# Two heads in one product: the low-order terms of a linear attention on stacked rows

## The reference

```
qn = _normalize(q) * (scale * temperature)
kn = _normalize(k) * scale
v1 = concat([ones, v]); vN = v1 / N
kv_mod = einsum('bhni,bhnj,bhne->bhije', kn, kn, vN)
kv     = einsum('bhnd,bhne->bhde', kn, vN)
vsum   = sum(vN, axis=-2)
y = A * einsum('bhni,bhnj,bhije->bhne', qn, qn, kv_mod) \
  + scale**2 * Bc * einsum('bhnd,bhde->bhne', qn, kv) + scale**4 * Cc * vsum
y = y[..., 1:] / y[..., :1]
```

## Time and profile before

| | |
|---|---|
| median of 3 runs | 958.41 us (952.2, 959.37, 958.41) |
| the profiled execution | 953.75 us, of which 951.9 us span |
| PE busy | 862.8 us (91%) |
| DVE busy | 645.4 us (68%) |
| ACT busy | 422.1 us (44%) |
| POOL busy | 711.0 us (75%) |
| mean granted TensorE clock | 0.94 |

### The profile page before, as it was taken

One profiled execution on the slowest core, in us unless ns is written; L12 is line 12 of the kernel. 1 busy time (PEld: TensorE's weight loads), 2 busy tenths in 40 slices (PEclk: granted clock), 3 DMA queues, 4 the chain that ended last, 5 costly groups with the idle time before them and its releaser, 6 DMA issues.

```text
span 951.9 us, 20339 instructions
## 1 busy us (share of the span) xinstructions
PE 862.8 (91%) x6492; PEld 533.1 (56%) x6492; DVE 645.4 (68%) x2267; ACT 422.1 (44%) x1156; POOL 711.0 (75%) x498
## 2 busy tenths in 40 slices
PE   3889997897999999999999999999969997599994
PEld 1434443344654554554554555556548986498993
DVE  3699998899487556556456566465886888655552
ACT  3545645333265333333433434344324555266763
POOL 4778878888888888888888888878633156677875
PEclk8699999898899899999999999999979998699997
DMA  9867586436565455445554565563566454578884
GB/s 300 187 134 143 77 166 108 65 42 108 70 123 99 52 85 86 65 42 86 97 86 51 95 102 93 91 124 29 104 199 218 134 193 151 175 125 138 136 134 56
DMA packets 148755, 108.72 MB, mean 114 GB/s; under 512 B 105223, under 2 KB 137162, under 8 KB 148524
## 3 DMA queue, kind: packets, MB, share of 16 engines
q0 software_dynamic: 61344, 26.21, 30.1%
q1 hardware_dynamic: 80800, 70.49, 26.3%
q10 hardware_dynamic: 6508, 10.73, 3.4%
HBM read 65.07 MB, written 42.45 MB: 113 GB/s over the span
## 4 chain that ended last, share of the span: by engine, by line
PE 76%; DVE 16%; issue 3%; DMA 2%; ACT 1%; SPq 0%; DVEq 0%; POOLq 0%; POOL 0%; ACTq 0%
PE ps L1416 15%; PE ps L1205 8%; DVE r2t L1744 6%; PE ps L1629 5%; PE ps L1352 5%; PE ps L1366 5%; PE ps L1640 5%; PE ps L1557 3%; PE ps L1243 3%; PE ps L1252 3%; PE ps L1403 3%; PE ps L1273 2%; PE ps L1392 2%; PE ps L1301 2%; DVE same L1684 2%
## 5 line engine op out<-in xcount | busy, mean ns | idle before, releaser
L748 POOL DMA_INDIRECT edge_sums<-sums,addr x352 | 553.2, 1572 | 126.1 <-issue 100.5
L1781 DVE TENSOR_SCALAR oh<-node,dsrc 128x500 bf16<-128x500 int16 (+1 forms) x448 | 134.5, 363 | 72.5 <-PE ps L1416 71.9
L1416 PE MATMUL ps<-oh,r2t 128*64 128x500 bf16 (+1 forms) x1344 | 146.6, 362 | 1.4 <-DVE oh L1781 1.4
L1003 ACT ACTIVATE r<-ps 128x500 f32<-128x500 f32 (+1 forms) x224 | 103.5, 550 | 80.1 <-PE ps L1352 79.9
L1416 PEld LDWEIGHTS ps<-oh,r2t 128*64 128x64 bf16 x1344 | 70.4, 111 | 72.9 <-issue 33.6
L1744 DVE TENSOR_TENSOR r2t<-ps,r 125x4096 f32<-125x4096 f32 x25 | 110.3, 4412 | 0.0
L1205 PEld LDWEIGHTS ps<-edges,same 128*128 128x128 f32 x704 | 89.3, 199 | 33.3 <-issue 30.1
L1205 PE MATMUL ps<-edges,same 128*128 128x65 f32 x704 | 98.4, 285 | 10.3 <-ACT sums L822 4.7
L793 POOL DMA_INDIRECT out_x<-r x56 | 87.8, 1568 | 26.6 <-DVE r L2179 9.5
L1684 DVE SCALAR_TENSOR_TENSOR same<-srow,src_f,below 128x128 f32<-128x128 int32 x352 | 101.0, 343 | 5.0 <-DMA srow<-in_src_row 5.0
L822 ACT ACTIVATE sums<-ps 128x260 f32<-128x260 f32 x88 | 35.1, 399 | 138.0 <-PE ps L1205 133.3
(11 more groups left out here) (300 smaller groups left out, 1382.4 us busy)
## 6 DMA issues: line engine op xcount, KB each, us to landing
srow<-in_src_row SPq DMA_DIRECT2D x44, 512.0 KB, 5.7
edges<-in_edge_attr SPq DMA_DIRECT2D x22, 512.0 KB
r<-routed_rows SPq DMA_DIRECT2D x56, 129.0 KB
r<-hpre_rows SPq DMA_DIRECT2D x12, 500.0 KB, 4.3
edge_sums<-sums,addr POOLq DMA_INDIRECT x352
r2t<-in_ew SPq DMA_DIRECT2D x4, 1024.0 KB, 10.9
hpre_rows<-r ACTq DMA_DIRECT2D x16, 250.0 KB, 2.6
edge_sums<-r SPq DMA_DIRECT2D x4, 884.0 KB, 13.3
```

What stands on the lines that cost most here:

```text
L748: pool.indirect_dma_start(out=tables[k], out_offset=bass.IndirectOffsetOnAxis(ap=addr[:, j:j + 1], axis=0), in_=sums[:, j % OR, :], in_off ...
L1003: act.activation(phT[:, R % 2, h, 0:n], bank(BP[h], 128, 0, n), ACT.Square).then_inc(pair_squares, 1)
L1416: m = mm(ps[EA * a:EA * (a + 1), BD * BANK:BD * BANK + n], lhsT=parts3[:, (DCH - 1 - 2 * w // DW) * DW + (2 * w + a) % DW, s, :], rhs=oh[: ...
L1781: v.tensor_scalar(oh[:, (2 * i + a) % OHS, 0:nt * P].rearrange("p (t n) -> p t n", t=nt), node16[:, 0:nt, :], dsrc[:, 2 * w + a:2 * w + a ...
```

## The change

The low-order terms of two heads are made by one product of 64 columns over 128 stacked rows: the two heads' queries on rows 0 to 63, their squares on rows 64 to 127. ScalarE builds these rows for both halves of a group, a copy and a square each, four instructions of 64 rows in place of one of 128. TensorE issues two such products, which write different halves of the PSUM rows. VectorE masks the weights in eight pieces of 64x64, which moves them to their rows, in place of two of 128x256.

```diff
-        wlow = sb("wlow", [128, HG, 2, 128])
+        wlow = sb("wlow", [128, HG, 2, 64])
-        R1 = 15800
+        R1 = 16300
-        qsq = carve([128, BW])
+        q_low = carve([128, 2, BW])
@@ q_squares
-                act.activation(qsq[:, 0:n], qnT[:, b % 2, g, 0:n], ACT.Square).then_inc(q2_ready, 1)
+                for a in range(2):
+                    here = qnT[64 * a:64 * a + 64, b % 2, g, 0:n]
+                    act.activation(q_low[0:64, a, 0:n], here, ACT.Copy)
+                    z = act.activation(q_low[64:128, a, 0:n], here, ACT.Square)
+                z.then_inc(q2_ready, 1)
@@ outputs
-                    wait(pe, low_ready, HG)
+                    wait(pe, low_ready, 4 * HG)
                     wait(pe, y_ready, HG * b + g)
                     wait(pe, q2_ready, HG * b + g + 1)
-                    mm(bank(BY, 128, 0, n), lhsT=wlow[:, g, 1, :], rhs=qnT[:, b % 2, g, 0:n], start=True, stop=False, skip_group_check=True)
-                    mm(bank(BY, 128, 0, n), lhsT=wlow[:, g, 0, :], rhs=qsq[:, 0:n], start=False, stop=False, skip_group_check=True)
+                    for a in range(2):
+                        mm(ps[64 * a:64 * a + 64, BY * BANK:BY * BANK + n], lhsT=wlow[:, g, a, :], rhs=q_low[:, a, 0:n], start=True, stop=False,
+                           skip_group_check=True)
@@ before the first gram product
-            pe.wait_ge(low_ready, HG)
+            pe.wait_ge(low_ready, 4 * HG)
@@ VectorE, once
-                v.tensor_tensor(wlow[:, g, :, :], bank(B1, 128, 2 * g * 128, (2 * g + 2) * 128).rearrange("p (a n) -> p a n", a=2),
-                                block[:, :, :].rearrange("p h d -> p (h d)").unsqueeze(1).to_broadcast([128, 2, 128]), ALU.mult).then_inc(low_ready, 1)
+                for a in range(2):
+                    rows = slice(64 * a, 64 * a + 64)
+                    mask = block[rows, 2 * a:2 * a + 2, :].rearrange("p h d -> p (h d)")
+                    for k in range(2):
+                        c0 = (2 * g + 1 - k) * 128 + 64 * a
+                        v.tensor_tensor(wlow[64 * k:64 * k + 64, g, a, :], ps[rows, B1 * BANK + c0:B1 * BANK + c0 + 64], mask,
+                                        ALU.mult).then_inc(low_ready, 1)
```

## The result

The changed kernel takes 964.76 us (median of 16 runs, 960.87 to 969.3), the kernel before 954.89 beside it (16 runs, 949.8 to 960.15): a ratio of 1.010, interval 1.0081 to 1.0118. The forecast was 960.4 with 954.5 to 967: the time lies in the range, but the kernel got slower by 9.9 us where the sum said 2.0. The profiled execution took 968.64 us, with 966.9 of span.

What follows compares the result with a forecast made beforehand. TensorE was taken to bound the attention stage. Its gain of 11.3 us less 5.0, 3.6, 1.8 and 0.7 of waits left about 0.2; with 2.2 for the clock, 958.41 became 960.4 us, range 954.5 to 967.

Steps and rivals of the forecast that it cites:

- round 0: sweep and sums copies: Blocks 1 to 6: ScalarE's longer work delays copies TensorE waits for, 5.0 us lost together.
- round 5: scaled queries, block 0's with them: TensorE waits longer for scaled queries: 3.6 us in blocks 1 to 5; block 0's gain of 0.90 lost too.
- masks: VectorE's eight 64x64 masks at 0.19 us each, 1.5 instead of 0.8 us; TensorE waits once, 0.7 us.
- clock: One or two further drops to half clock behind round 0 stalls, most likely in block 3; 2.2 us taken.
- The low pair: TensorE's two 64-column products run side by side: 0.98 us per wide group, 0.77 per narrow one.
- Rival (d): TensorE's two low products don't run side by side and cost 1.88 us as before: 967 us, chance 0.05.
- I take 4 x 0.51 = 2.04, that is 1.53 us more per wide group: ScalarE's four 64-row pieces cost 0.51 us each, half rows saving nothing; 1.21 us more per narrow group.
- both waits hang on VectorE's row, not on the low products: Block 0, rounds 1 and 5: TensorE's gain, 2 x 0.90 = 1.8 us, just turns into longer waits.
- Rival (a): No further clock drop, as the new stalls stay shorter than those of blocks 1 and 2: 958.2 us, chance 0.22.
- rival (c): The clock drops in every round 0, 7 to 10 us: 965 to 968, say 967 us, chance 0.15.
- The ceiling of 3.1 us: Stage end: the fourth table lands at 700.7, so at most 3.1 us of TensorE's saving arrive; losses arrive whole.
- Rival (b): ScalarE's delay doesn't reach TensorE, as half rows cost less or pieces overlap more: 955.3 us, chance 0.13.

Runs made afterwards that it cites:

- e1: Changed kernel with ScalarE's four instructions moved behind the copies in round 0 and the next block's query squares in round 4; 949.54 us, 0.9937 of the kernel before.
- e4: Changed kernel plus end series of four ScalarE instructions, varying row count, function, row shift and source; four from SBUF on 64 unchanging rows took 2.13 to 2.15 us.
- e9: Changed kernel plus end series of four 64-row ScalarE instructions whose input or output rows alternate; 2.5 us for four, 2.26 with a single change.
- e11: Changed kernel with only round 4's four ScalarE instructions moved, behind the next block's query squares; 962.75 us, 1.0093 of the kernel before.
- e8: e1 with the masks in four instructions of 64x128 in place of eight of 64x64; 951.25 us, 0.9951 of the kernel before.
- e10: Changed kernel with only round 0's four ScalarE instructions moved behind the rest of that round, blocks 1 to 6; 957.13 us, 1.0016 of the kernel before.

## Why the prediction was nearly right, and where its sum was too small

| step, us | predicted | in the changed kernel's profile |
|---|---|---|
| TensorE's work | -11.3 | -11.4 (e1, at an equal time of half clock) |
| round 0: sweep and sums copies | +5.0 | 4.5 + 7.8 - 4.7 = +7.6 |
| round 5: scaled queries, block 0's with them | +3.6 + 0.9 | 8.7 - 0.9 = +7.8 |
| block 0, round 1: one-hots | +0.9 | 2.2 - 1.4 = +0.8 |
| masks | +0.7 | +1.3 |
| clock | +2.2 | +5.8 |
| sum | +2.0 | +11.9 |

The sum is that of one pair of profiles, whose stage grew by 11.7 us; the medians are 9.9 apart. The mechanism was the one forecast: TensorE saves 11 us and gives them back as waits in the same block, only that it gives back 17.5 us and not 11.1. Shown by e1: the waits went with the place of the instructions.

That the time fell into the range is partly luck. The sum was put on the median of three runs, 958.41, and 16 runs have 954.89, 3.5 us less. On that base the forecast would have been 956.9 and the range 951.0 to 963.5, and 964.76 lies outside. Over 1 per cent slower had a chance of 0.06, and the ratio is 1.010.

By steps:

- **The low pair** (0.98 and 0.77 predicted) took 0.99 in a wide and 0.79 in a narrow block (544.15 to 544.94 in block 4). Rival (d) is out.
- **"I take 4 x 0.51 = 2.04, that is 1.53 us more per wide group"**: the term that was mis-sized. Half the rows do cost as much as all (e4), but the four don't overlap, as each changes rows (e9): 2.02 more in a wide block, and 1.72 (0.40 before, 2.12 now) instead of 1.21 in a narrow one. 0.5 us in six rounds 0 is 3 us, about the 2.6 by which that row fell short; the rounds 5 of blocks 1 to 5 bear it too.
- **"both waits hang on VectorE's row, not on the low products"**: false for block 0's round 5. VectorE's row begins with the next block's squares on ScalarE, there as in the other blocks. L889 follows the start of the four by 2.53 us, before by 1.34 (284.09 to 285.43): 1.19 late, and with the gain of 0.89 that is 2.08 of the 2.25 that the wait grew.
- **The masks** cost 0.25 us apiece, not 0.19: nearer to the middle of the bounds than to the short end that I chose.
- **The clock**: two drops more, as said, in block 3 and, not forecast, in block 0; those of blocks 1 and 2 came again and block 2's grew from 3.4 to 6.8 us. Over the runs of a kernel they vary, so this term is a spread more than a number. Rival (a), no further drop, is out in this profile. The falls of rival (c), behind nearly every round 0, came in e11; the changed kernel comes near that rival's 965 with a fall in only one of the blocks 3 to 6 of its profile.
- **The ceiling of 3.1 us** holds for no loss and so wasn't tested by the change; as a bound it was too low. e1 saved 6.8 us of 956.38. The bound took the table's landing at 700.7 as fixed, and it isn't: it came at 699.8 in e1's profile and at 697.7 in that of e8, whose stage begins at 239.7, as early as before, and there the table was added at 698.12, 5.7 us earlier than before. Nor do the scatters run free of the other engines: late sums copies held them up, and the table of the changed kernel landed at 710.2.
- **Rival (b)**, that ScalarE's delay doesn't reach TensorE, is out. Its reason, that half the rows cost less or overlap more, fails in e4 and e9; the delay stayed away from TensorE only where the work was moved (e1, 0.9937).

The Trainium skill (TensorE: Matmul & The Clock Gate, Why this matters for your kernels) warns of long idle gaps between bursts of products. Block 0's round 5, a gap of 3.20 us, agrees; block 3 fell behind 1.37 us all the same, and e10's behind no gap, so here the measurement decides.

## What to carry to other kernels

What an added instruction costs in this kernel is decided by what stands behind it on its queue: the same four cost 1.6% ahead of a copy that TensorE waits for and nothing measurable behind it. So before shortening work on the busiest engine by giving work to an idle one, look for the first consumer of the new result (here a whole round later) and put the work as late as that allows. Price it by the spacing of like instructions on like rows, and follow each chain back past the engine that a wait names to where it begins.

## What was not expected of the hardware

In these series from SBUF, ScalarE starts an instruction 0.51 us after the one before if both use the same rows, and 0.63 if the rows read or written differ, 500 columns each; whether 64 or 128 rows are used makes no difference. Most of the spread between runs of one kernel goes with the granted clock: of the 20 runs of the kernel before beside e1, the two at a mean clock of 0.946 and 0.947 took 950.25 and 950.57 us, the five at 0.936 took 957.36 to 960.2, and the one at 0.933 957.3. And falls to half clock came behind light products with a wait of 1.37 us, of 0.98, and with none; what decides between a fall and none at the same place in two executions was not settled.
